# Slot rows stored by slot and gathered by token onto x, in place of scatter-adds into a copy of x

## The chip, the cores and the metric

The kernel runs on one core of a Trainium2 chip. The metric is the device time of one launch in microseconds; smaller is better. The core's engines run side by side and are tied by semaphores: TensorE (PE), VectorE (DVE), ScalarE (ACT), GpSimd (POOL) and SyncE (SP), which here only issues DMAs. ACT and POOL issue DMAs too; only POOL can issue indexed ones and ones that add to their destination.

## The reference

Four layers, each added to x (2048 tokens of 512 values, float32) through a gate:

```python
x = x + tanh(g_xattn[0]) * L0_xattn(layernorm(x), ids, ctx)      # per token one of 4 experts
x = x + tanh(g_ffn[0])   * L0_ffn(layernorm(x), w_gate, w_up, w_down)  # quantized FFN
x = x + tanh(g_xattn[1]) * L1_xattn(layernorm(x), ctx, ctx, gamma)
x = x + tanh(g_ffn[1])   * L1_ffn(layernorm(x), ...)             # 64 experts, top 6
```

The first layer picks an expert e by token id; with h = layernorm(x) it gives silu(h ctx[e]^T) * (h ctx[e]^T) ctx[e]^T for that token. The second quantizes activations and weights in blocks of 32 to a tiny float with a shared exponent. The change touches the end of the first layer and the start of the second. The third and fourth stay as they are.

## The kernel before

**Layer 1, in slots.** The tokens are sorted by expert into 19 slots of 128 rows; a slot belongs to one expert, and the last rows of an expert's last slot can be empty. DVE computes slot[p, i], the slot row of token 128 i + p, and token[p, j], the token of row p in slot j. For each slot j: POOL gathers the tokens' rows of x into hin (gather(j), L593, five slots ahead); DVE measures them (L907); POOL makes the deviations (L600 to L602); ACT normalises; TensorE turns them (turn_h, L1284) and multiplies by ctx (z, L1295); ACT's silu and DVE's product give prod (L913); TensorE turns it (turn_a, L1304) and multiplies again (y, L1311); ACT scales the result into ysb (L1662, signals y_out). POOL then scatters ysb to DRAM (scatter(j), L624): an indirect DMA that adds the 128 rows to x_sum, a tensor of 2048 + 19 x 128 rows. Its first 2048 rows are a copy of x, made by four DMAs on ACT's queue (L1690) at 24 us; empty rows go to the rest, by the index tile target, which DVE makes after token (five small instructions).

**The weights of layer 2** are quantized in the same slots, as 16 tiles; a slot j with j % 4 != 3 has one. SP loads a tile (load_w, L491 to L493, three DMAs of 256 KB, two tiles ahead, after POOL's wy_ready); DVE finds the largest values (L871) and the scales (L877, L880); POOL multiplies (normal, L608); ACT squares (L1668); DVE pushes and pulls (L886 to L898); TensorE turns the tile (turn_w, L1321); ACT writes it to SLAB.

**Hand-over.** When all scatters have landed, SP loads x_sum's first 2048 rows as 16 DMAs of 256 KB into X (L512). X held ctx until about 18 us and is free in between.

**Layer 2, in 16 tiles of tokens.** enter(i) measures X[i] on DVE (L949), deviation_x makes the deviations on POOL (L647 to L650, four small instructions), ACT normalises (L1717), measure_h finds the block scales on DVE (L957 to L959), and POOL's normal_h (L655), DVE's cast (L965) and POOL's back_h (L660) quantize. TensorE turns (L1358) and multiplies (L1366). The product's two halves h are quantized too: measure_i on DVE (L979 to L981), normal_i on POOL (L665), cast_i on DVE (L986), back_i on POOL (L671), then TensorE turns them (L1377) and multiplies down (L1385); DVE's leave adds to X (L991).

The order on each engine is the order in which the code is written; an engine waits at each instruction for its semaphores, and nothing behind it can overtake. POOL's order in step i of layer 2 is back_i(i-1,1), back_h(i+1), deviation_x if i is odd (up to i = 11), normal_i(i,0), normal_h(i+2), back_i(i,0), normal_i(i,1).

## Time and profile before

| | us |
|---|---|
| median of 3 runs | 1050.43 (1050.4 to 1052.26) |
| the profiled execution | 1051.51, of which span 1049.8 |
| PE busy | 973.2 (93%) |
| POOL busy | 639.8 (61%) |
| DVE busy | 632.5 (60%) |
| ACT busy | 420.8 (40%) |
| slots of layer 1 | about 24 to 205 |
| layer 2 | about 210 to 435 |

An engine's share is a mean over stages with different limits. A row of the timeline gives the start and the duration of an instruction (or of several of one kind), its engine and line, what it writes and reads, and in brackets how long the engine was idle before it and what ended that. A DMA's row on its issuing engine is the time to issue it; its landing is told apart. For POOL that time is the making of its descriptors.

### The profile page before, as it was taken

The page shows a single profiled execution, that of the slowest core. Times are in us where ns is not written, and L with a number is a line of the kernel's source. Part 1 is how long each engine was busy: PE and PEld are TensorE (multiplying, and loading weights), DVE is VectorE, ACT ScalarE, POOL GpSimd, SP SyncE. Part 2 cuts the span into 40 slices and gives each one's busy share as a digit, 9 for nine tenths or more (in the row PEclk, how much of TensorE's full clock was granted, in tenths as well). Part 3 has the DMA queues.
Part 4 walks back from the last instruction along what each step waited for, and adds up shares of the span by engine and source line. Part 5 has one row for each costly group of instructions (what it writes and reads, how often), then busy time and mean ns, then how long its engine had stood idle before and what let it go on. Part 6 is the DMA issues. An engine that isn't in the chain of part 4 may idle for free.

```text
span 1049.8 us, 13677 instructions
## 1 busy us (share of the span) xinstructions
PE 973.2 (93%) x4436; PEld 474.9 (45%) x4436; DVE 632.5 (60%) x1168; ACT 420.8 (40%) x817; POOL 639.8 (61%) x565
## 2 busy tenths in 40 slices
PE   6699999969999999799999999999999999999992
PEld 4355555424444444344444445335455555555530
DVE  5478876868888887577777777981222222222221
ACT  4466565434444444466666665332111111111100
POOL 4399996558888887686766661245444554445430
PEclk9899999989999999899999999999999999999996
DMA  9555555240000001230001605178999999999848
GB/s 310 190 131 142 122 144 115 48 143 1 1 1 1 2 1 41 81 130 21 21 23 36 234 1 201 30 259 272 331 336 333 340 335 335 338 335 334 242 63 182
DMA packets 64148, 162.90 MB, mean 155 GB/s; under 512 B 9888, under 2 KB 10032, under 8 KB 63632
## 3 DMA queue, kind: packets, MB, share of 16 engines
q1 hardware_dynamic: 47488, 116.94, 31.9%
q0 software_dynamic: 16464, 40.91, 18.1%
q10 hardware_dynamic: 128, 4.19, 1.2%
q8 instruction: 37, 0.61, 0.2%
q14 instruction: 31, 0.25, 0.1%
HBM read 129.67 MB, written 39.67 MB: 161 GB/s over the span
## 4 chain that ended last, share of the span: by engine, by line
PE 64%; POOL 14%; DVE 8%; issue 7%; DMA 4%; ACT 2%; SPq 0%; POOLq 0%; DVEq 0%; ACTq 0%
PE PS L1580 15%; PE PS L1599 8%; PE PS L1424 6%; PE PS L1401 6%; PE PS L1412 6%; POOL ARENA L665 6%; PE PS L1311 5%; PE PS L1295 5%; POOL ARENA L671 3%; PE PS L1569 3%; PE PS L367 3%; DVE ARENA L986 2%; POOL ARENA L660 1%; DMA XNT<-in_L_ffn_w_down 1%; DVE ARENA L1195 1%
## 5 line engine op out<-in xcount | busy, mean ns | idle before, releaser
L715 POOL TENSOR_TENSOR ARENA<-ARENA 128x512 f32<-128x512 f32 x128 | 133.3, 1063 | 55.8 <-DVE ARENA L1021 55.7
L1366 PE MATMUL PS<-SLAB,ARENA 128*128 128x512 bf16 x512 | 118.8, 382 | 12.6 <-DVE ARENA L972 10.9
L761 POOL DMA_INDIRECT out<-ARENA,idx x32 | 46.2, 1445 | 124.4 <-DVE ARENA L1227 106.8
L1855 ACT ACTIVATE ARENA<-PS 96x192 f32<-96x192 f32 x64 | 20.9, 327 | 226.4 <-PE PS L1580 186.3
L1227 DVE COPY ARENA<-PS 96x512 f32<-96x512 f32 x64 | 41.1, 682 | 94.6 <-PE PS L1599 94.6
L1762 ACT ACTIVATE ARENA<-PS,ARENA 128x512 f32<-128x512 f32 x128 | 86.8, 683 | 23.1 <-DVE ARENA L1015 19.8
L1015 DVE TENSOR_REDUCE ARENA<-PS 128x2 f32<-128x1024 f32 x64 | 78.2, 1222 | 9.3 <-PE PS L1401 9.1
L1366 PEld LDWEIGHTS PS<-SLAB,ARENA 128*128 128x128 bf16 x512 | 48.4, 98 | 75.0 <-issue 21.5
L1580 PE MATMUL PS<-SLAB,ARENA 128*96 128x384 f32 x240 | 81.0, 490 | 0.0
L1412 PEld LDWEIGHTS PS<-ident,ARENA 128*128 128x128 f32 x512 | 54.8, 141 | 51.1 <-issue 36.6
L1728 ACT ACTIVATE ARENA<-PS 128x512 f32<-128x512 f32 x64 | 38.2, 597 | 97.5 <-PE PS L1366 97.5
L671 POOL TENSOR_TENSOR ARENA<-ARENA 128x1024 bf16<-128x1024 fp8e4 x32 | 61.1, 1911 | 24.3 <-DVE ARENA L986 24.3
L665 POOL TENSOR_TENSOR ARENA<-ARENA 128x1024 f32<-128x1024 f32 x32 | 62.8, 1962 | 20.0 <-DVE ARENA L981 20.0
L754 POOL DMA_INDIRECT ARENA<-rows,idx x64 | 60.3, 942 | 23.3 <-issue 11.0
L1401 PE MATMUL PS<-ARENA 64*128 64x512 f32 x256 | 73.6, 652 | 0.2 <-ACT ARENA L1762 0.2
L1311 PE MATMUL PS<-CT,XNT 128*128 x152 | 70.9, 610 | 2.2 <-ACT XNT L1657 1.7
L1412 PE MATMUL PS<-ident,ARENA 128*128 128x128 f32 x512 | 70.7, 280 | 1.7 <-DVE XNT L1028 1.7
L1295 PE MATMUL PS<-CT,ARENA 128*128 x152 | 68.5, 593 | 1.6 <-ACT ARENA L1647 1.6
L1424 PE MATMUL PS<-XNT,CT 128*64 128x512 f32 x256 | 68.2, 616 | 0.0
L1215 DVE SCALAR_TENSOR_TENSOR ARENA<-PS,ARENA 96x192 f32<-96x192 f32 x64 | 26.2, 409 | 69.2 <-ACT ARENA L1855 62.8
L1385 PE MATMUL PS<-SLAB,ARENA 128*128 128x512 bf16 x256 | 62.0, 387 | 0.0
L1771 ACT ACTIVATE XNT<-PS 128x512 f32<-128x512 f32 x64 | 38.2, 597 | 53.2 <-PE PS L1412 53.1
(267 smaller groups left out, 1868.3 us busy)
## 6 DMA issues: line engine op xcount, KB each, us to landing
SLAB<-in_L_ffn_w_gate SPq DMA_DIRECT2D x30, 384.0 KB
SLAB<-in_L_ffn_w_up SPq DMA_DIRECT2D x30, 384.0 KB
X<-in_L_ffn_w_down SPq DMA_DIRECT2D x14, 768.0 KB
SLAB<-in_L_ffn_w_down SPq DMA_DIRECT2D x10, 768.0 KB
CT<-in_L_ffn_w_gate SPq DMA_DIRECT2D x16, 384.0 KB
CT<-in_L_ffn_w_up SPq DMA_DIRECT2D x16, 384.0 KB
X<-in_ctx SPq DMA_DIRECT2D x4, 1024.0 KB, 5.5
XNT<-in_L_ffn_w_gate SPq DMA_DIRECT2D x16, 256.0 KB
```

Of the source, the lines that this page charges most:

```text
L665: pool.tensor_tensor(blocks(iy[:, h, :]), blocks(inter[:, par, h, :]), spread(iinv[:, h, :]), ALU.mult).then_inc(iy_ready, 1)
L671: pool.tensor_tensor(blocks(qi[:, par, h, :]), blocks(ic[:, h, :]), spread(im[:, par, h, :]), ALU.mult).then_inc(iq_ready, 1)
L715: last = pool.tensor_tensor(prob[s % 4][:, h, :], prob[s % 4][:, h, :], rec[:, s % 4, h:h + 1].to_broadcast([P, D]), ALU.mult)
L1295: last = pe.matmul(bank(2 + j % 2), hT[:, j % 2, k * P:(k + 1) * P], CT[:, bass.ds(e, 1), k, :].rearrange("p a s -> p (a s)"), start=(k == ...
L1311: last = pe.matmul(bank(4 + j % 2), aT[:, j % 2, k * P:(k + 1) * P], CT[:, bass.ds(e, 1), k, :].rearrange("p a s -> p (a s)"), start=(k == ...
L1366: last = pe.matmul(bank(b), QT[:, par, k * P:(k + 1) * P], w[:, k, c * D:(c + 1) * D], start=(k == 0), stop=(k == KD - 1))
L1401: last = pe.matmul(bank(2 * (s % 2) + h), qn[rows_h, i % 2, c * P:(c + 1) * P], keys4[rows_h, i % 4, :], start=True, stop=True)
L1412: last = pe.transpose(bank(4 + h)[:, k * P:(k + 1) * P], prob[s % 4][:, h, k * P:(k + 1) * P], ident[:, :])
L1424: last = pe.matmul(bank(6 + i % 2)[h * DH:h * DH + DH, :], CT[:, b, k, r * P + h * DH:r * P + h * DH + DH], PT[h][i % 2][:, k, :], start=( ...
L1580: last = pe.matmul(bank(2 + e % 2)[0:CAP, 0:2 * F1].rearrange("p (n f) -> p n f", n=2), bT[:, e % 2, k, :], gate_up_of(e)[:, :, k, :], sta ...
L1599: last = pe.matmul(bank(4 + n)[0:CAP, :], hT6[half, t % 2, m, :], down_of(t)[half, m, :], start=(m == 0), stop=(m == 2))
L1762: last = act.activation(prob[s % 4][:, h, :], bank(2 * (s % 2) + h), ACT.Exp, bias=nmax[:, s % 4, h:h + 1], accum_out=esum[:, s % 4, h:h + 1])
```

## The change

- x_sum becomes slot_out, a tensor of 19 x 128 rows in the order of the slots. The copy of x on ACT's queue goes, and so do target, pads and target_ready.
- SP stores each slot's ysb to slot_out with a plain DMA (store_y). The store of slot j-1 stands in SP's order behind the weight tile of slot j; behind it stands the weight tile of slot j+1.
- SP loads x itself into X, eight DMAs of 512 KB, in slots 1 to 8.
- POOL's scatters go from the slots. After its last weight tile POOL waits for X and all stores and gathers slot_out by slot[:, i] onto X[:, i, :] with an indirect DMA that adds (gather_x): four at once, number 4 before normal_h(0), number 5 before normal_h(1), then two at the end of each of the steps 0 to 4.
- The matmuls that find token have 38 columns in place of 57.

The weight tiles stay in the slots in which they were.

```diff
+                def store_y(j):
+                    sp.wait_ge(y_out, j + 1)
+                    sp.dma_start(slot_out_v[:, j, :], ysb[:, j % 2, :]).then_inc(y_stored[j % 2], 16)
+
                 for j in range(SLOTS):
                     if j in TILED and tile_at(j) + 2 < NT:
                         load_w(tile_at(j) + 2)
-
-                sp.wait_ge(y_stored[0], 16 * ((SLOTS + 1) // 2))
-                sp.wait_ge(y_stored[1], 16 * (SLOTS // 2))
-                for i in range(NT):
-                    need(sp, yg_in[i % 4], 16 * (i // 4))
-                    sp.dma_start(X[:, i, :], x_sum_v[:, i, :]).then_inc(yg_in[i % 4], 16)
+                    if 1 <= j <= NT // 2:
+                        need(sp, c_turned, NT)
+                        sp.dma_start(X[:, 2 * j - 2:2 * j, :], x_v[:, 2 * j - 2:2 * j, :]).then_inc(x_in, 16)
+                    if j:
+                        store_y(j - 1)
+                store_y(SLOTS - 1)
...
-                    pool.indirect_dma_start(x_sum, bass.IndirectOffsetOnAxis(ap=target[:, j:j + 1], axis=0),
-                                            ysb[:, j % 2, :], None, compute_op=ALU.add).then_inc(y_stored[j % 2], 16)
...
+                def gather_x(i):
+
+                    need(pool, yg_in[i % 4], 16 * (i // 4))
+                    pool.indirect_dma_start(X[:, i, :], None, slot_out, bass.IndirectOffsetOnAxis(ap=slot[:, i:i + 1], axis=0),
+                                            compute_op=ALU.add).then_inc(yg_in[i % 4], 16)
+
+                pool.wait_ge(x_in, 16 * (NT // 2))
+                pool.wait_ge(y_stored[0], 16 * ((SLOTS + 1) // 2))
+                pool.wait_ge(y_stored[1], 16 * (SLOTS // 2))
+                for i in range(4):
+                    gather_x(i)
                 deviation_x(0, 1)
                 deviation_x(1, 1)
+                gather_x(4)
                 normal_h(0)
                 back_h(0, 0)
                 deviation_x(2, 2)
+                gather_x(5)
                 normal_h(1)
...
                     if live(i, 0):
                         back_i(i, 0, par)
                         normal_i(i, 1, par)
+                    for g in range(2 * i + 6, min(2 * i + 8, NT)):
+                        gather_x(g)
...
-                for b in range(B):
-                    act.dma_start(x_sum[b * S:(b + 1) * S, :], x_rows[b * S:(b + 1) * S, :]).then_inc(x_in, 16)
```

SP's order in slots 1 to 3. In the kernel before, weight tiles 3, 4 and 5 follow each other (L491 to L493, here tile 3 and the first DMA of tile 4):

```order
L491 DMA XNT<-in_L_ffn_w_gate 128x512
L492 DMA XNT<-in_L_ffn_w_up 128x512
L493 DMA XNT<-in_L_ffn_w_down 128x512
L491 DMA XNT<-in_L_ffn_w_gate 128x512
L492 DMA XNT<-in_L_ffn_w_up 128x512
```

After the change, from tile 3 on (L512 loads x, L505 stores a slot):

```order
L489 DMA XNT<-in_L_ffn_w_gate 128x512
L490 DMA XNT<-in_L_ffn_w_up 128x512
L491 DMA XNT<-in_L_ffn_w_down 128x512
L512 DMA X<-in_x 128x2x512
L505 DMA slot_out<-ARENA 128x512
L489 DMA XNT<-in_L_ffn_w_gate 128x512
L490 DMA XNT<-in_L_ffn_w_up 128x512
L491 DMA XNT<-in_L_ffn_w_down 128x512
L512 DMA X<-in_x 128x2x512
L505 DMA slot_out<-ARENA 128x512
L512 DMA X<-in_x 128x2x512
L505 DMA slot_out<-ARENA 128x512
```

Between two weight tiles there is now a load of x and one or two stores, each store with a wait for y_out.

POOL's order in step 0 of layer 2 and the head of step 1, before: normal_i(0,0), normal_h(2), back_i(0,0), normal_i(0,1), back_i(0,1), back_h(2).

```order
L665 TENSOR_TENSOR ARENA<-ARENA 128x1024
L655 TENSOR_TENSOR ARENA<-ARENA 128x512
L671 TENSOR_TENSOR ARENA<-ARENA 128x1024
L665 TENSOR_TENSOR ARENA<-ARENA 128x1024
L671 TENSOR_TENSOR ARENA<-ARENA 128x1024
L660 TENSOR_TENSOR ARENA<-ARENA 128x512
```

The same place after the change (normal_i is L655 there, normal_h L645, back_i L661, back_h L650, gather_x L667):

```order
L655 TENSOR_TENSOR ARENA<-ARENA 128x1024
L645 TENSOR_TENSOR ARENA<-ARENA 128x512
L661 TENSOR_TENSOR ARENA<-ARENA 128x1024
L655 TENSOR_TENSOR ARENA<-ARENA 128x1024
L667 DMA X<-slot_out,slot 128x512 x2
L661 TENSOR_TENSOR ARENA<-ARENA 128x1024
L650 TENSOR_TENSOR ARENA<-ARENA 128x512
```

Two gathers now stand between normal_i(0,1) and back_i(0,1); steps 1 to 4 have the same.

## Rows read from the trace of the kernel before

**Rows 1.** Busy time by stretch: engines with counts, PE clock, DMA share, GB/s.

```profile
core 0: us, PE busy (x) PEld busy (x) DVE busy (x) ACT busy (x) POOL busy (x), PEclk, DMA share, GB/s
60.00:70.00 10.00, 10.00 (x56) 6.05 (x55) 7.61 (x8) 7.08 (x12) 9.05 (x8) 1.00 0.58 155
```

**Rows 2.** The chain of waits, slots 1 and 2: start us, us, what.

```profile
52.13 4.65 PE PS L1311 x8
56.78 3.43 PE PS L1295 x8
60.22 0.44 PE PS L1304 x4
...
61.76 3.49 PE PS L1311 x8
```

**Rows 3.** Timeline of DVE around weight tiles 1 and 2.

```profile
24.92 1.75 DVE L871 TENSOR_REDUCE ARENA<-XNT 128x48 f32<-128x1536 f32 x1 [4.00 <-DMA XNT<-in_L_ffn_w_down]
...
29.65 0.19 DVE L880 TENSOR_SCALAR ARENA<-ARENA 128x48 int16<-128x48 int16 x1
42.42 1.75 DVE L871 TENSOR_REDUCE ARENA<-XNT 128x48 f32<-128x1536 f32 x1 [12.58 <-DMA XNT<-in_L_ffn_w_down]
```

**Rows 4.** Timeline of SP's queue: first DMA of tile 1, last of tile 2.

```profile
18.33 0.33 SPq L491 DMA_DIRECT2D XNT<-in_L_ffn_w_gate  x1
...
27.07 0.49 SPq L493 DMA_DIRECT2D XNT<-in_L_ffn_w_down  x1
```

**Rows 5.** DMA queues from 20 to 45 us: packets, MB, share of 16 engines.

```profile
q10 hardware_dynamic: 128, 4.19, 49.4%
```

**Rows 6.** Timeline of TensorE, the turns of prod(1).

```profile
45.62 1.11 PE L1304 MATMUL PS<-ident,XNT 128*128 128x128 f32 x4 [4.13 <-DVE XNT L913]
```

**Rows 7.** Timeline of POOL, steps 4 and 5 of layer 2.

```profile
279.49 1.92 POOL L665 TENSOR_TENSOR ARENA<-ARENA 128x1024 f32<-128x1024 f32 x1 [1.09 <-DVE ARENA L981]
...
285.33 2.02 POOL L665 TENSOR_TENSOR ARENA<-ARENA 128x1024 f32<-128x1024 f32 x1 [0.39 <-DVE ARENA L981]
288.16 1.91 POOL L671 TENSOR_TENSOR ARENA<-ARENA 128x1024 bf16<-128x1024 fp8e4 x1 [0.81 <-DVE ARENA L986]
...
292.72 1.92 POOL L665 TENSOR_TENSOR ARENA<-ARENA 128x1024 f32<-128x1024 f32 x1
```

**Rows 8.** Timeline, slots 2 to 4: a weight load, y_out(2), DVE's next measurement.

```profile
63.06 0.33 SPq L491 DMA_DIRECT2D XNT<-in_L_ffn_w_gate  x1
...
65.89 0.70 ACT L1662 ACTIVATE ARENA<-PS,tgate 128x512 f32<-128x512 f32 x1
...
75.85 0.69 DVE L907 BATCH_NORM_STATS2 ARENA<-ARENA 128x6 f32<-128x512 f32 x1 [2.08 <-DMA ARENA<-in_x,ARENA]
```

**Rows 9.** Lines 593 (gathers) and 624 (scatters): POOL's time and the landing.

```profile
L593 POOL DMA_INDIRECT ARENA<-in_x,ARENA x19: 945/1032/2610, 14.4 to 158.0; - x19
...
DMA to landing us min/median/max: 4.2/5.4/6.2
...
L624 POOL DMA_INDIRECT x_sum<-ARENA x19: 1585/1663/3264, 54.0 to 201.8; - x19
...
DMA to landing us min/median/max: 4.7/6.0/7.3
```

**Rows 10.** Timeline of the hand-over: last y_out, first enter, first measure_h.

```profile
200.79 0.70 ACT L1662 ACTIVATE ARENA<-PS,tgate 128x512 f32<-128x512 f32 x1
...
210.25 0.69 DVE L949 BATCH_NORM_STATS2 ARENA<-X 128x6 f32<-128x512 f32 x1 [3.81 <-DMA X<-x_sum]
...
213.64 0.69 DVE L957 TENSOR_REDUCE ARENA<-ARENA 128x16 f32<-128x512 f32 x1
```

**Rows 11.** Line 549, twelve plain stores of 256 KB from X to DRAM: landing.

```profile
DMA to landing us min/median/max: 2.0/2.4/3.0
```

**Rows 12.** Line 789, direct DMAs of 256 rows that add, on POOL.

```profile
L789 POOL DMA_DIRECT2D out<-SLAB x2: 1182/1206/1231, 1032.0 to 1035.1; - x2
```

**Rows 13.** Timeline of DVE beside the first scatter.

```profile
53.93 1.75 DVE L886 SCALAR_TENSOR_TENSOR ARENA<-ARENA,XNT 128x1536 f32<-128x1536 bf16 x1
```

**Rows 14.** Timeline of TensorE, the last turns of layer 2, after a wait each.

```profile
425.29 0.62 PE L1377 MATMUL PS<-ident_b,ARENA 128*128 128x128 bf16 x8 [2.09 <-POOL ARENA L671]
...
430.30 1.03 PE L1377 MATMUL PS<-ident_b,ARENA 128*128 128x128 bf16 x8 [2.89 <-POOL ARENA L671]
```

More of the change, by code:

```diff
@@ L102, in build @@
     slot_in = nc.dram_tensor("slot_in", [SLOTS * P, D], F32, kind="Internal").ap()
[L103 removed]
+    slot_out = nc.dram_tensor("slot_out", [SLOTS * P, D], F32, kind="Internal").ap()
     rows = nc.dram_tensor("rows", [ROWS, RW], F32, kind="Internal").ap()
@@ L236, in build @@
         x_rows = x.rearrange("b s d -> (b s) d")
-        x_sum_v = x_sum[0:T, :].rearrange("(i p) d -> p i d", p=P)
+        slot_out_v = slot_out.rearrange("(j p) d -> p j d", p=P)
         def blocks(a, n=BLK):
@@ L639, in _ @@
                     normal(n)
-                scatter(SLOTS - 1)
                 def deviation_x(i, n):
```

24 lines of the change are left out of this document (3 added, 21 removed).

## The prediction

> **What bounds the kernel now.** I read the busy table in slices of 10 us first, then the chain of waits from 0 to 300 us, then the timelines of the engines at the places where the chain leaves TensorE. Only the first 430 us matter: what follows does not touch x_sum, the scatters or X's loading, and moves as a block. All times below are on the clock of the kernel before.
>
> The expert slots (24 to 205 us) are bound by TensorE once they run: it is busy 10.00 of 10 us, at full clock, while DVE has 7.61 and the DMA engines 0.58 [rows 1]. A full slot of the chain is z (3.43), four turns of prod and h (0.44 each), twelve of the weight tile and y (3.49) [rows 2]. Before they run there is one stall. DVE is free at 29.84 and its next instruction, the largest values of weight tile 2 (L871), begins at 42.42, after 12.58 us of idle that ended with the tile's DMA [rows 3]. The last of its three DMAs was issued at 27.07 [rows 4]. Between 20 and 45 us the copy of x into x_sum (queue q10, 4.19 MB) held 49.4% of the 16 engines, 12.4 us of 25 [rows 5]. TensorE waits from 45.62 - 4.13 = 41.49, the end of z(2), for prod(1), which stands behind L871 on DVE [rows 6]; it then waits again for the tile's own transposes. Its matmuls after that run slowly: y(1) takes 4.65 us where a later y takes 3.49 [rows 2].
>
> In the quantized FFN (218 to about 425 us) the chain of waits goes POOL, DVE, POOL. In a step, normal_i(i,0) (L665), back_i(i,0), normal_i(i,1), back_i(i,1) (L671) are tied by a DVE cast or measurement between each two. The last of these gaps is 0.81 us on POOL [rows 7]. back_i(i,1) is issued at the head of step i+1, and behind it stand back_h, four small instructions if i+1 is odd, and normal_i(i+1,0). With the four small ones POOL comes to normal_i(i+1,0) without a gap (292.72); without them it waits 1.09 us (279.49) [rows 7]. So time put on POOL between normal_i(i,1) and back_i(i,1) is hidden for 0.81 us if i is even, for 0.81 + 1.09 = 1.90 us if it is odd, and lengthens the FFN beyond that.
>
> **Part 1, the copy of x goes (gain).** Four DMAs leave ACT's queue. x now comes to SBUF as eight loads of 512 KB in slots 1 to 8. Weight tile 2 is asked for from 26.1 on and then lands by 33: tile 1 was asked for at 18.33 and used at 24.92, 6.6 us later, with five gathers beside it [rows 3, 4]. TensorE ends z(2) at 41.49 and goes on: 41.49 + (61.76 - 60.22 = 1.54 of turns) = 43.03, where y(1) begins, + 3.49 = 46.53, where z(3) begins. DVE does not hold it: from L871 to y(1) all that hangs on tile 2 took 52.13 - 42.42 = 9.71 us [rows 2, 3], and 33 + 9.71 = 42.7. Before, z(3) begins at 56.78 [rows 2]. Gain 10.25 us, of which 1.2 is the y at full clock. Each us by which tile 2 lands after 33.3 costs one; I take 9 to 10.5 as bounds. The slots behind it are tied to TensorE and keep the gain.
>
> The X loads use the same engines. A slot's share is 0.58 now [rows 1]; they add at most 12.4 / 8 = 1.5 us of engine time to each of eight slots of 3.43 + 3.49 + 1.54 = 8.46 us, 0.18, and the scatters leave. So nothing waits there. The Trainium skill (DMA: Bandwidth & Descriptors, Issuing engines are not separate DMA queues) says the same of the mechanism: transfers from SP, ACT and POOL run on the same engines and interleave. By it the 12.4 us of engine time are only moved, and the sum would lose what part of them meets a busy engine.
>
> **Part 2, scatters become stores.** Nineteen scatters leave POOL's slot stage (1.59 to 3.26 us each [rows 9]); POOL is not on the chain there, 0. Each store is now an SP instruction that waits for y_out(j), and behind it stand the next three weight DMAs. After a slot without a tile the load is then later than today: SP issues at 63.06, while y_out of slot 2 comes at 65.89 + 0.70 = 66.59 [rows 8]. Tile 5 lands some 3.5 us later, about 1 us behind the time DVE takes it; DVE then idles 2.08 us in that slot anyway [rows 8]. Four such slots: 0, with 4 x 0.5 as the bad bound. Five small DVE instructions and a third of the columns of the matmuls at 13 us leave as well; DVE then waits 2 us for tile 0 anyway: 0.
>
> **Part 3, the hand-over.** Before, y_out(18) ends at 200.79 + 0.70 = 201.49, its scatter and X's first load follow, and DVE measures tile 0 at 210.25 and begins measure_h(0) (L957) at 213.64 [rows 10]. After: SP issues the store at about 201.6; a 256 KB store lands in 2.4 us (2.0 to 3.0) [rows 11], 204.0. Then POOL issues four gathers that add into X.
>
> **What is such a gather's price?** The trace has no gather with an add. Plain gathers of the same 128 rows cost POOL 0.945 at least, 1.03 in the median; scatters with the add 1.585 at least, 1.66 in the median. They land in 4.2 to 6.2 and 4.7 to 7.3 us [rows 9]. A direct DMA with the add costs 1.2 [rows 12]. I take 1.60, since it is the row with both properties, indexed and adding; 1.03 stays the low end. Landing 4.7. Between two of them stand 0.3 us, as between two plain ones.
>
> Gather 3 is issued at 204.0 + 3 x 1.9 = 209.7 and lands at 214.4; enter(3) takes 0.9, so measure_h(0) begins at 215.3: 1.7 us later than before. With 1.03 and 4.2 it is 204.0 + 4.0 + 4.2 + 0.9 = 213.1, 0.5 earlier; with 1.66 and 7.3, 4.5 later. POOL's two deviations wait behind the gathers but end before measure_h(0). Gathers 4 and 5 fall where POOL waits in any case: 0.
>
> **Part 4, ten gathers inside FFN steps 0 to 4.** Each of these steps has two, right before back_i(i,1). A pair costs 0.17 + 1.60 + 0.30 + 1.60 + 0.07 = 3.74. Steps 0, 2 and 4 hide 0.81: 3 x 2.93 = 8.8. Steps 1 and 3 hide 1.90: 2 x 1.84 = 3.7. Sum 12.5 us. TensorE waits for back_i(i,1) with its transposes, has nothing to do meanwhile, and the stage never gets it back, since later steps have the same tie. With 1.03 a pair is 2.60: 3 x 1.79 + 2 x 0.70 = 6.8. With 2.2 (a DVE instruction beside it) it is 4.94: 3 x 4.13 + 2 x 3.04 = 18.5.
>
> On that last price: the first scatter, at 54.0, is the longest, 3.26 us in place of 1.60 [rows 9], and beside it runs a DVE instruction with two inputs in SBUF (L886) [rows 13]. The Trainium skill (SBUF — State Buffer, Who interferes with whom) has the rule: DVE and GpSimd hold a shared port pair exclusively, and a DMA issued from GpSimd can't write its descriptors meanwhile. The rows agree. By that rule the casts beside a pair could cost a gather up to their own length. In the FFN, DVE has one cast beside a pair and no instruction like L886; I take nothing for it in the sum.
>
> **Sum.** -10.25 + 1.7 + 12.5 = +3.95 us. The profiled execution took 1051.51 (span 1049.8), 1.1 above the median of 1050.43; the change is made against itself, so 1050.4 + 4.0 = **1054.4 us**.
>
> **The rivals.**
> (a) The gather is cheap. It counts as a gather, not as a scatter: 1.03 to 1.2 us. Then -10.25 - 0.5 + 6.8 = -3.95 at 1.03, 1046.5 us; at 1.2 (pair 2.94: 3 x 2.13 + 2 x 1.04 = 8.5, hand-over +0.3) it is -1.5, 1049. This one ends faster. It decides below 1.15 us a gather. For it: plain gathers hardly grow with rows, and a direct add of 256 rows costs 1.2 [rows 12]. Against it: the only indexed adds in the trace are the dear ones.
> (b) The clock falls. After a wait of 2.89 us in TensorE, eight transposes took 1.03 us, after one of 2.09 only 0.62 [rows 14]; a pair of gathers leaves it about 3 us without work. With the 1.16 us that y(1) lost to the same cause, a fallen clock costs some 0.41 + 1.16 = 1.6 us a step, less what the chain covers (up to 0.8). In three to five steps 3 to 7 us on top of the forecast: 1057 to 1061.
> (c) The front stays. If tile 2 still lands at 42 or another wait takes L871's place (an SP wait, a gather of h), part 1 gives nothing or half: 1059 to 1065. The timeline speaks against it: all else that DVE and TensorE need then is there by 38.
>
> **Chances.** Forecast (1052.5 to 1057.5) 0.40; (a) 0.42, of which 0.24 with 1.03 and 0.18 with 1.2; (b) 0.12; (c) 0.06. So the forecast is the likeliest of the prices. A difference of 0.2%, 2.1 us, is about what a measurement of this kernel can tell from none. Faster by more than that: 0.32, nearly all of (a) at 1.03, a third of (a) at 1.2; within it 0.21, the rest of (a) and the forecast's low edge; slower 0.47. The range runs from the low end of (a), with another 1.5 us for the front, to the middle of (b) and of the cheaper (c): 1045.0 to 1060.0; the forecast's own is 1052.5 to 1057.5.
>
> **What the profile after would show.** Right: no wait of DVE for tile 2 over 3 us, TensorE busy without a hole from 34 us on, z(3) about 10 us earlier; POOL's DMA_INDIRECT into X near 1.6 us; measure_h(0) 8.5 us earlier than 213.64, not 10; back_i(i,1) behind two gathers in five steps, periods near 16 and 14.6 us there in place of 13.2 and 12.7. Wrong: gathers near 1.0 (then a); L1377 at 1.0 in steps 1 to 5 (then b); a wait of 5 us or more in TensorE before 60 (then c), or TensorE waiting for tiles 5, 8, 11 or 14, which would make the SP order dear.

## The result, and the profile after

| | before | after |
|---|---|---|
| median of 4 runs each, us | 1051.35 (1050.4 to 1052.29) | 1060.13 (1059.27 to 1060.85) |
| the profiled execution, us | 1051.51 | 1059.75 |
| its span, us | 1049.8 | 1057.8 |
| ratio of the runs, 95% interval | | 1.0075 (1.0062 to 1.0088) |

The changed kernel is slower, by 8.0 us of span, 8.2 us of profiled time and 8.8 us between the medians (7.9 us by the ratio); the forecast was +3.95. The sign and the mechanism came as forecast, and the size is twice that.

**The front.** The timeline of DVE after, the largest values of weight tiles 1, 2 and 3 (start us, us, what; in brackets the idle time before and what ended it):

```profile
24.70 1.75 DVE L869 TENSOR_REDUCE ARENA<-XNT 128x48 f32<-128x1536 f32 x1 [3.64 <-DMA XNT<-in_L_ffn_w_down]
31.80 1.75 DVE L869 TENSOR_REDUCE ARENA<-XNT 128x48 f32<-128x1536 f32 x1 [1.35 <-DMA XNT<-in_L_ffn_w_down]
40.37 1.75 DVE L869 TENSOR_REDUCE ARENA<-XNT 128x48 f32<-128x1536 f32 x1
```

The second row is tile 2: it waited 1.35 us where [rows 3] show 12.58. TensorE then has no hole (timeline of TensorE, y(1) and z(3)):

```profile
43.48 3.65 PE L1309 MATMUL PS<-CT,XNT 128*128 x8
46.97 3.60 PE L1293 MATMUL PS<-CT,ARENA 128*128 x8
```

z(3) begins 9.81 us earlier than in [rows 2]. The gain is kept: y_out(18) ends at 191.14 + 0.70 = 191.84 us, 9.65 before that of [rows 10].

**The hand-over.** POOL, DVE and TensorE in order of time: the four gathers (L667), the last enter, measure_h(0) (L955), the first turns and products of the FFN (L1356, L1364) and the first normal_i (L655):

```profile
194.65 1.85 POOL L667 DMA_INDIRECT X<-slot_out,slot  x1 [6.37 <-DMA slot_out<-ARENA]
...
200.53 1.54 POOL L667 DMA_INDIRECT X<-slot_out,slot  x1 [0.30 <-issue]
...
205.98 0.69 DVE L947 BATCH_NORM_STATS2 ARENA<-X 128x6 f32<-128x512 f32 x1 [1.36 <-DMA X<-slot_out,slot]
...
206.81 0.65 DVE L955 TENSOR_REDUCE ARENA<-ARENA 128x16 f32<-128x512 f32 x1
...
210.65 0.61 PE L1356 MATMUL PS<-ident_b,ARENA 128*128 128x128 bf16 x4 [7.68 <-POOL ARENA L650]
212.04 9.69 PE L1364 MATMUL PS<-SLAB,ARENA 128*128 128x512 bf16 x32 [0.78 <-ACT ARENA L1719]
...
222.09 1.91 POOL L655 TENSOR_TENSOR ARENA<-ARENA 128x1024 f32<-128x1024 f32 x1 [5.21 <-DVE ARENA L979]
```

measure_h(0) is 6.83 us earlier than in [rows 10], so the hand-over took 2.8 of the 9.65. normal_i(0,0) is only 5.55 earlier (227.64 before): another 1.3 went in the first products, which took 9.69 us in place of 8.38.

**The steps.** POOL in step 0 and at the head of step 1: normal_i(0,1), the pair of gathers, back_i(0,1), back_h(1), and, behind four small instructions, normal_i(1,0):

```profile
227.93 2.02 POOL L655 TENSOR_TENSOR ARENA<-ARENA 128x1024 f32<-128x1024 f32 x1 [0.39 <-DVE ARENA L979]
230.10 2.04 POOL L667 DMA_INDIRECT X<-slot_out,slot  x1 [0.15 <-issue]
232.44 1.55 POOL L667 DMA_INDIRECT X<-slot_out,slot  x1 [0.30 <-issue]
233.43 2.51 POOL L661 TENSOR_TENSOR ARENA<-ARENA 128x1024 bf16<-128x1024 fp8e4 x1
235.30 1.64 POOL L650 TENSOR_TENSOR ARENA<-ARENA 128x512 bf16<-128x512 fp8e4 x1
...
238.64 1.90 POOL L655 TENSOR_TENSOR ARENA<-ARENA 128x1024 f32<-128x1024 f32 x1
```

normal_i(i,0) begins at 222.09, 238.64, 252.95, 269.85, 284.17 and 300.85 us, so the five steps take 16.55, 14.31, 16.90, 14.32 and 16.68 us, where they took 13.25, 12.67, 13.24, 12.69 and 13.23: +13.7 in all. Shift by shift: -9.65 at y_out(18), -6.83 at measure_h(0), -5.55 at normal_i(0,0), +8.1 at normal_i(5,0), +8.0 at the end. From step 5 on the kernel moves as a block but for small shifts that cancel: +6.9 behind the end of layer 2, where the last sixteen products down took 5.27 us before and 4.45 after (TensorE's granted clock was 0.70 in the kernel before from 433 to 439 us), and +8.0 again at the end.

(The start that the trace gives a POOL instruction right behind a gather is too early: L661 "begins" at 233.43 while the gather runs to 233.99. Its end, 235.94, fits the instructions behind it. So sums over steps go by ends or by rows further on. Two of the starts above, 252.95 and 284.17, are of this kind: the instructions last 2.5 us there and 1.9 elsewhere. By the ends of normal_i(i,0) the five steps are longer by 3.3, 2.2, 3.1, 2.2 and 2.8 us.)

### The profile page after: what moved, and what is told of

The parts are those of the page before. It is cut to its first block, busy times and chain, and to the rows that moved or that the text cites. A ratio compares the mean times of both kernels' runs of the same rounds, so it can differ in the third digit from the quotient of the medians.

```text
span 1057.8 us, 13675 instructions
## 1 busy us (share of the span) xinstructions
PE 973.7 (92%) x4436; PEld 475.7 (45%) x4436; DVE 632.3 (60%) x1163; ACT 420.0 (40%) x817; POOL 631.8 (60%) x562
## 4 chain that ended last, share of the span: by engine, by line
PE 65%; POOL 15%; DVE 7%; issue 7%; DMA 2%; ACT 2%; POOLq 0%; DVEq 0%; ACTq 0%; SPq 0%
PE PS L1578 15%; PE PS L1597 8%; PE PS L1293 6%; PE PS L1422 6%; PE PS L1399 6%; PE PS L1410 6%; PE PS L1309 6%; POOL ARENA L655 6%; POOL ARENA L661 4%; PE PS L1567 3%; PE PS L365 3%; DVE ARENA L984 2%; POOL X L667 2%; POOL ARENA L650 1%; DVE ARENA L1193 1%
## 5 line engine op out<-in xcount | busy, mean ns | idle before, releaser
L1364 PE MATMUL PS<-SLAB,ARENA 128*128 128x512 bf16 x512 | 119.6, 385 | 10.5 <-DVE ARENA L970 8.8
L1364 PEld LDWEIGHTS PS<-SLAB,ARENA 128*128 128x128 bf16 x512 | 49.0, 99 | 72.8 <-issue 19.0
L611 POOL TENSOR_TENSOR XNT<-XNT,ARENA 128x1536 f32<-128x1536 f32 x16 | 45.6, 2851 | 52.3 <-DVE ARENA L878 52.1
L661 POOL TENSOR_TENSOR ARENA<-ARENA 128x1024 bf16<-128x1024 fp8e4 x32 | 63.5, 1986 | 20.5 <-DVE ARENA L984 20.5
L655 POOL TENSOR_TENSOR ARENA<-ARENA 128x1024 f32<-128x1024 f32 x32 | 63.9, 1998 | 17.2 <-DVE ARENA L979 17.2
L759 POOL DMA_INDIRECT ARENA<-rows,idx x64 | 60.0, 938 | 23.7 <-issue 11.3
L1383 PE MATMUL PS<-SLAB,ARENA 128*128 128x512 bf16 x256 | 64.9, 400 | 0.0
```

Of the source, the lines that this page charges most:

```text
L655: pool.tensor_tensor(blocks(iy[:, h, :]), blocks(inter[:, par, h, :]), spread(iinv[:, h, :]), ALU.mult).then_inc(iy_ready, 1)
L661: pool.tensor_tensor(blocks(qi[:, par, h, :]), blocks(ic[:, h, :]), spread(im[:, par, h, :]), ALU.mult).then_inc(iq_ready, 1)
L1364: last = pe.matmul(bank(b), QT[:, par, k * P:(k + 1) * P], w[:, k, c * D:(c + 1) * D], start=(k == 0), stop=(k == KD - 1))
```

## The experiments

Each is compared with the kernel before on the same chip at the same time. One thing must be known to read the profiled times: z(0), the first product, takes 3.69 us in some executions and 5.39 in others, whatever the kernel. In the long ones TensorE's granted clock falls to half during it (0.50 from 25 to 28 us in the profile of the copy by rows, 1.00 throughout in that of the kernel before). Of the thirteen profiles, seven have 5.39, and all that follows in them is 1.7 us later. The kernel before was profiled with 3.69, the changed kernel too. It may be what sets the two levels of the runs of before (1050.4 and 1052.3); that was not shown.

### Part 1 by itself

The kernel before without the copy and with scatters that write:

```diff
-                for b in range(B):
-                    act.dma_start(x_sum[b * S:(b + 1) * S, :], x_rows[b * S:(b + 1) * S, :]).then_inc(x_in, 16)
...
-                                            ysb[:, j % 2, :], None, compute_op=ALU.add).then_inc(y_stored[j % 2], 16)
+                                            ysb[:, j % 2, :], None).then_inc(y_stored[j % 2], 16)
```

> The kernel before without the copy of x and with scatters that write in place of adding (it leaves out the addition of x to the first layer's result). All else stands. This is part 1 of the prediction by itself. Theory: -9.7 to -10.3 from the front, nothing else on the path but the last scatter, which without the add costs POOL about 0.5 us less: 1051.3 - 10 - 0.5 = 1040.8, bounds 1039.5 to 1042.5. Rival (the front gains less than 9 us, the rest of the changed kernel's loss being smaller than I read it): 1043 to 1047. The price of a scatter without add: 0.95 to 1.1 us if the add is what is dear, 1.6 if it is the direction.

Measured: 1039.14 us against 1053.02, ratio 0.9871 (0.9854 to 0.9887), 13.9 us faster, more than I had expected (my lower bound was 1039.5). Its timelines:

```profile
46.93 3.60 PE L1294 MATMUL PS<-CT,ARENA 128*128 x8
...
192.07 1.93 POOL L623 DMA_INDIRECT x_sum<-ARENA  x1 [3.83 <-ACT ARENA L1661]
...
202.38 0.65 DVE L956 TENSOR_REDUCE ARENA<-ARENA 128x16 f32<-128x512 f32 x1
```

z(3) at 46.93 is that of the changed kernel (46.97), and so is the last y_out, whose instruction on ACT begins at 191.10 (191.14). So the front of the change is the copy and nothing else, -9.7 us. Of the rest I had expected 0.5 us: measure_h(0) is 11.3 us earlier than in [rows 10], 1.6 more than the front. A scatter that writes lands sooner: SP, which waits for it, issues X's first load 195.77 - 192.07 = 3.70 us after the scatter began, in place of 207.36 - 201.76 = 5.60. POOL's part of that is 1.93 us in place of 2.51; the remainder, 1.77 in place of 3.09, is on the way to memory. So at this place adding costs there too, not only on POOL. The profiled span gained 12.6 us: 11.3 up to normal_i(5,0) (281.45 in place of 292.72), and most of the other 1.3 at the end of layer 2, in the products at a lower clock named above.

The price of a scatter without the add was to be read here as well. The quickest took 1.01 us on POOL in place of 1.585, so the add is what is dear in this direction too. But the median was 1.93, more than the 1.66 of the scatters with the add [rows 9]: in the slots what runs beside a scatter counts for more than the add.

### The price of the add

The changed kernel, with gathers that overwrite:

```diff
-                    pool.indirect_dma_start(X[:, i, :], None, slot_out, bass.IndirectOffsetOnAxis(ap=slot[:, i:i + 1], axis=0),
-                                            compute_op=ALU.add).then_inc(yg_in[i % 4], 16)
+                    pool.indirect_dma_start(X[:, i, :], None, slot_out, bass.IndirectOffsetOnAxis(ap=slot[:, i:i + 1], axis=0)).then_inc(yg_in[i % 4], 16)
```

> The changed kernel, with the sixteen gathers of slot_out writing X in place of adding to it (it leaves out the addition of x after the first layer). Everything else stands. Theory (the add is the price): POOL needs 1.0 to 1.1 us a gather in place of 1.57, as for the plain gathers of h; a step with a pair gets 1.0 to 1.3 us shorter, the hand-over 1.5 to 2.5: 1060.1 - 5 x 1.15 - 2 = 1051.5 to 1054.5. Rival (the indexed read into X or the place in the program is the price): gathers stay at 1.5 or more, 1059 to 1061.

Measured: 1050.14 us against 1052.36, ratio 0.9988 (0.9977 to 0.9999), some 9 to 10 us under the changed kernel and 1.4 under my range. Line 667 (POOL's time min/median/max in ns, then the landing) in the changed kernel, and then in this one:

```profile
L667 POOL DMA_INDIRECT X<-slot_out,slot x16: 1539/1568/2112, 194.7 to 294.7; - x16
...
DMA to landing us min/median/max: 4.6/5.0/5.7
```

```profile
L667 POOL DMA_INDIRECT X<-slot_out,slot x16: 946/1035/1525, 194.5 to 285.3; - x16
...
DMA to landing us min/median/max: 3.4/3.6/4.0
```

The add costs 0.53 us of POOL and 1.4 us of landing for each gather. This is the point on which the forecast and rival (a) parted: with the price of a plain gather (1.03) the change would have been about level with the kernel before. The two terms shrink where they should: the five steps lengthen by 7.35 us in place of 13.7, and normal_i(0,0) comes at 218.78, 3.3 us earlier. I had given the hand-over 1.5 to 2.5 us of this; that the landing gets shorter as well I had left out.

### Part 4 by itself

The changed kernel without the ten late gathers (DVE's enter waits for x alone from tile 6 on):

```diff
-                    for g in range(2 * i + 6, min(2 * i + 8, NT)):
-                        gather_x(g)
```

> The changed kernel without the ten gathers of steps 0 to 4 (it leaves out the first layer's result for tiles 6 to 15); the six before the FFN stay. Theory: all of the lengthening of steps 0 to 4 (3.30, 1.64, 3.66, 1.63, 3.45 us, 13.7 in all) is the gathers on POOL: 1060.1 - 13.7 = 1046.4, with 1045.5 to 1047.5 as bounds, periods of 13.2 and 12.7 us, and a full TensorE clock from 225 us on. Rival (part of it is TensorE's fallen clock from the hand-over, or DMA traffic, which stays without them): 1048 to 1052.

Measured: 1046.38 us against 1052.36, ratio 0.9940 (0.9920 to 0.9960). Against the changed kernel's 1.0075 that is 1.35%, 14.2 us, and the spans differ by 14.1 (its z(0) took 5.39 us, its first products 8.57 in place of 9.69, so the gathers' price is better read from the periods). POOL's normal_i(i,0) begins at 222.77, 236.04, 248.70, 262.11, 274.78 and 288.01: periods of 13.27, 12.66, 13.41, 12.67 and 13.23, those of the kernel before within 0.2 us in all. So the 13.7 us are the gathers.

### Where in a step POOL's time is free

The ten late gathers one to a step, the same number at the same place:

```diff
-                    for g in range(2 * i + 6, min(2 * i + 8, NT)):
-                        gather_x(g)
+                    if i + 6 < NT:
+                        gather_x(i + 6)
```

> The changed kernel, with the ten late gathers one to a step (number i + 6 at the end of step i, steps 0 to 9) in place of two in steps 0 to 4. The number of gathers, their price and their place in a step are the same. Theory (each step hides what POOL waits anyway before back_i(i,1) and, if i is odd, before the next normal_i as well: 0.81 and 1.90 us): one gather with its gaps is 1.84 (2.3 where it takes 2.04); five even steps cost 1.03 to 1.5 each, five odd ones 0 to 0.4. So +5.2 to +9.5 in place of +13.7: 1051.6 to 1056, best 1052.5. Rival (ten gathers cost what they cost, nothing is hidden): 1060. Second rival (shorter waits of TensorE also keep its clock full): up to 1 us less than the theory's sum.

Measured: 1054.00 us against 1053.02, ratio 1.0010 (1.0001 to 1.0020). Nearly 7 us of the ten gathers' cost is gone, with all ten still there. The even steps and the odd ones part as the model has it (POOL, the gathers of steps 0 to 2 and normal_i(i,0) of steps 0 to 3):

```profile
223.94 1.91 POOL L655 TENSOR_TENSOR ARENA<-ARENA 128x1024 f32<-128x1024 f32 x1 [5.49 <-DVE ARENA L979]
...
231.96 2.04 POOL L667 DMA_INDIRECT X<-slot_out,slot  x1
238.65 1.90 POOL L655 TENSOR_TENSOR ARENA<-ARENA 128x1024 f32<-128x1024 f32 x1
...
246.69 2.10 POOL L667 DMA_INDIRECT X<-slot_out,slot  x1 [0.18 <-issue]
251.31 2.30 POOL L655 TENSOR_TENSOR ARENA<-ARENA 128x1024 f32<-128x1024 f32 x1
...
259.72 1.60 POOL L667 DMA_INDIRECT X<-slot_out,slot  x1 [0.15 <-issue]
265.97 1.90 POOL L655 TENSOR_TENSOR ARENA<-ARENA 128x1024 f32<-128x1024 f32 x1
```

A pair of steps takes 265.97 - 238.65 = 27.32 us from an odd step's head on, where it took 25.9. Two gathers of 2.10 and 1.60 with their gaps are 4.2 us of POOL, and 2.71 (0.81 + 1.90) of that is hidden: 1.5 is left, 1.4 measured. The rival (a gather costs what it costs) is out.

### The clock at the head of the FFN

Five more matmuls that nobody reads:

```diff
-                unread(6)
+                unread(11)
```

> The changed kernel, with five more of the matmuls that nobody reads (L1325, 0.43 us each) after the last weight tile, so that TensorE is idle 5.5 us before the first transposes of the FFN, as in the kernel before (5.18), and not 7.68. Theory (the 1.3 us that the first step lost come from the clock, which rises later: gate_up of tile 0 took 9.69 us in place of 8.38): gate_up(0) back to 8.4 us, normal_i(0,0) 1.3 us earlier, 1058.8. Rival (gather 5, which stands between the deviations and normal_h(1), is what delays the first step, and the clock is no cause): 9.69 stays or falls without any gain, 1060.1.

Measured: 1059.91 us against 1053.02, ratio 1.0062 (1.0037 to 1.0086). The theory (1058.8 in place of 1060.1) stood for a ratio near 1.0062 and the rival for 1.0075. The interval holds both, so the times decide nothing.

The trace of the changed kernel decides on the rival. The first transposes were released by back_h(0,0), which ended at 210.60, before gather 5 began (212.50); TensorE was busy without a gap in the products; and normal_i(0,0) followed their end by 0.36 us, as in the kernel before. Gather 5 held up nothing here. The 1.3 us are TensorE's clock, which the changed kernel shows as follows (length, busy TensorE, its granted clock in shares of 2.4 GHz, DMA share, GB/s):

```profile
208.00:209.00 1.00, 0.00 (x0) 0.50 0.84 135
...
216.00:217.00 1.00, 1.00 (x4) 0.50 0.63 113
217.00:218.00 1.00, 1.00 (x5) 0.81 0.00 0
218.00:219.00 1.00, 1.00 (x7) 1.00 0.00 0
```

Whether a longer wait cost more of it is another matter. This is what the thirteen profiles have (TensorE's idle time before the FFN's first transposes, these four transposes, and the 32 products behind; where one of the products is missing from the trace, 31):

| kernel | wait, us | transposes, us | products, us |
|---|---|---|---|
| last slot sooner (below) | 1.01 | 0.40 | 6.85 (31) |
| DVE adding out of PSUM (below) | 2.64 | 0.40 | 8.54 (31) |
| no copy | 3.55 | 0.40 | 8.27 |
| five more matmuls (this run) | 3.85 | 0.40 | 8.18 (31) |
| rows of x kept (below) | 4.26 | 0.61 | 9.30 (31) |
| overwriting gathers | 4.41 | 0.45 | 9.93 |
| before | 5.18 | 0.61 | 8.38 |
| copy behind the tile (below) | 5.29 | 0.60 | 9.55 |
| copy by rows (below) | 5.43 | 0.61 | 9.97 |
| after | 7.68 | 0.61 | 9.69 |
| six gathers | 7.98 | 0.61 | 8.57 |
| one gather a step | 8.04 | 0.61 | 9.60 (31) |
| direct adds (below) | 8.50 | 0.60 | 8.89 (31) |

From 4.26 us on the length says nothing: the products take 8.4 to 10.0 us in no order, and two kernels that are the same up to this place, with waits of 7.98 and 8.04 us, took 8.57 and 9.60. In the three profiles with waits of 2.64 to 3.85 us the transposes still ran at full clock; the clock fell to half behind them, and the products took 8.2 to 8.5. After 1.01 us it didn't fall at all. So the 1.3 us lie within what this place varies by from profile to profile, and that the longer wait of the changed kernel caused them is not shown. Nor is it refuted: this run's edit brought the wait to 3.85 us, and its products are among the quick ones.

### Why the copy held weight tile 2

Two versions of the kernel before that keep copy, scatters and hand-over. The first names the rows:

```diff
-                    act.dma_start(x_sum[b * S:(b + 1) * S, :], x_rows[b * S:(b + 1) * S, :]).then_inc(x_in, 16)
+                    act.dma_start(x_sum_v[:, 4 * b:4 * b + 4, :], x_v[:, 4 * b:4 * b + 4, :]).then_inc(x_in, 16)
```

> The kernel before, with one edit: the four DMAs of the copy of x name their rows (128 x 4 rows of 2 KB each) in place of one contiguous MB each. In the kernel before the copy went as 128 packets of 32 KB, the weight tile beside it in packets of 2 KB. Theory (packet size): an engine takes the queues in turn, one packet each, so a weight row waits for a 32 KB packet each time; with packets of 2 KB tile 2 gets its share, lands by about 33 us, and DVE's wait for it falls from 12.58 us to under 4. Then TensorE goes on as in the changed kernel, and the time is 8 to 10 us under the kernel before: 1041.5 to 1043.5. Rival (bytes): 4.2 MB ahead of the tile keep the engines full for 12 us however they are cut; the wait stays at 9 to 12.6 us and the time at 1048 to 1052. A second rival: the copy by rows is itself slower and scatter 0 waits for it on POOL, which gives part of the gain back: 1044 to 1048.

Measured: 1046.32 us against 1052.36, ratio 0.9944 (0.9928 to 0.9961). DVE's row for tile 2 and the queues from 20 to 46 us (packets, MB, share of 16 engines), first before, then here:

```profile
q10 hardware_dynamic: 128, 4.19, 47.5%
q1 hardware_dynamic: 1295, 2.36, 26.5%
```

```profile
37.49 1.75 DVE L871 TENSOR_REDUCE ARENA<-XNT 128x48 f32<-128x1536 f32 x1 [5.82 <-DMA XNT<-in_L_ffn_w_down]
...
q10 hardware_dynamic: 2112, 4.19, 47.5%
q1 hardware_dynamic: 1292, 2.35, 26.3%
```

The copy took the same share of the engines, but tile 2 landed 10.3 us after its last issue in place of 15.3. DVE's wait fell from 12.58 us to 5.82, where it is 1.35 without a copy: packets of 2 KB in place of 32 KB give back six tenths of the stall. The rest stays, which speaks for the bytes. Neither theory was right alone. The time lies in the range of the second rival, but not for its reason: POOL issued scatter 0 after 0.17 us of idle time, so it didn't wait for the copy, though the copy's four DMAs landed later (13.6 us in the median in place of 10.0). As a change to the kernel this line gives 6 us at no cost.

The second moves the copy behind tile 2 on SP's queue:

```diff
                         load_w(tile_at(j) + 2)
+                    if j == 0:
+                        for b in range(B):
+                            sp.dma_start(x_sum[b * S:(b + 1) * S, :], x_rows[b * S:(b + 1) * S, :]).then_inc(x_in, 16)
```

> The kernel before, with the same copy of x (contiguous, 32 KB packets) issued by SP right behind weight tile 2 on SP's queue, not by ACT ahead of it. It takes the front of the change alone: scatters, x_sum and the loads of X by SP stay. Theory: tile 2 lands before 33 us, DVE's wait for it is under 4 us, TensorE has no hole at 41 us; but tile 3, asked for near 33 us, now stands behind the copy until about 43, some 3 us later than DVE wants it, and scatter 0 holds POOL until the copy has landed. Gain 6 to 9.5: 1042 to 1045.5. Rival (the stall only moves to tile 3 or to POOL behind scatter 0): gain 0 to 4, 1047 to 1051.

Measured: 1049.32 us against 1052.36, ratio 0.9968 (0.9955 to 0.9980). Tile 2 came in time, and tile 3, which now stood behind 4 MB, became the stall:

```profile
31.86 1.75 DVE L874 TENSOR_REDUCE ARENA<-XNT 128x48 f32<-128x1536 f32 x1
...
48.98 1.75 DVE L874 TENSOR_REDUCE ARENA<-XNT 128x48 f32<-128x1536 f32 x1 [7.12 <-DMA XNT<-in_L_ffn_w_down]
```

Its last DMA landed 13.4 us after its issue. The rival had this right: most of the stall only moves.

### Towards a kernel that is faster than both

The front gives 9.7 us and the ten gathers take more than that back. Four kernels try to have the first without the second.

**Scatters that write, then eight direct adds.** X is loaded from x in the slots, POOL scatters by token without add, and adds x_sum's rows onto X by ordinary DMAs of 256 rows:

```diff
+                def add_y(g):
+                    need(pool, yg_in[g % 4], 16 * (g // 4))
+                    pool.dma_start(X[:, 2 * g:2 * g + 2, :], x_sum_v[:, 2 * g:2 * g + 2, :], accum_op=ALU.add).then_inc(yg_in[g % 4], 16)
```

> Half of each kernel: no copy of x, SP loads x into X in slots 1 to 8 as in the changed kernel; POOL scatters each slot by token as in the kernel before, but without the add (nothing has to be there first); after the last one POOL adds the rows onto X with eight direct DMAs of 256 rows (two at once, one before normal_h(0), one before normal_h(1), one at the end of steps 1, 3, 5 and 7). Theory (an add of 256 contiguous rows costs POOL 1.2 us as at the kernel's end, 1.7 beside a cast of DVE, and odd steps hide 1.9): front -9.6 and hand-over -1.9 as in the kernel without the copy, +2 to +4 for the add in place of SP's load, 0 in the steps: 1052.5 - 13.9 + 3 = 1041.6, bounds 1039.5 to 1044. Rival (the add itself lands late, 8 to 12 us as the two at the kernel's end, 11.4 to 12.0 us): the hand-over loses 6 to 9 us, 1045 to 1048.

Measured: 1047.63 us against 1051.62, ratio 0.9962 (0.9948 to 0.9976). The steps cost nothing, as expected: normal_i(1,0) at 238.70, (2,0) at 251.37, (3,0) at 264.62, with an add of 1.26 us in step 1. The loss is at the hand-over: the adds were issued at 199.67, DVE had tile 0 only at 205.87, 6.2 us later, and tile 2 at 208.96. From the last scatter's start to measure_h(0) it took 15.2 us, 4.9 more than with SP's loads in the kernel without the copy. That is less than the rival's 6 to 9 and more than my 2 to 4; the time is in the rival's range.

**The rows of x kept in SBUF.** Each slot's rows of x are gathered anyway, for the normalisation. Here they go into X, which is free, and stay there; no copy of x is needed, since POOL adds them onto ysb before a scatter that writes:

```diff
-                    pool.indirect_dma_start(hin[:, j % HR, :], None, x_rows,
+                    pool.indirect_dma_start(X[:, j % NT, :], None, x_rows,
...
+                    own.link(pool.tensor_tensor(ysb[:, j % 2, :], ysb[:, j % 2, :], X[:, j % NT, :], ALU.add))
                     pool.indirect_dma_start(x_sum, bass.IndirectOffsetOnAxis(ap=target[:, j:j + 1], axis=0),
-                                            ysb[:, j % 2, :], None, compute_op=ALU.add).then_inc(y_stored[j % 2], 16)
+                                            ysb[:, j % 2, :], None).then_inc(y_stored[j % 2], 16)
```

> The kernel before, without the copy of x: each slot's rows of x are gathered into X (free until the hand-over) and stay there; ACT normalises from X into hin; POOL adds them onto ysb (128 x 512, some 1.05 us) and scatters without add into x_sum; SP loads X at the hand-over as before. Theory (the copy is the whole cost of the front, and an indirect DMA without add is cheap on POOL in this direction too, 0.95 to 1.1 us): DVE's wait for tile 2 under 3.5 us, z(3) near 47, so -9.7; POOL has in a slot 2.76 + 1.05 + 1.05 + 1.07 + 1.0 = 6.9 of 8.46 us, so the slots stay bound by TensorE; the last scatter comes 1.1 us later and costs 0.5 less. 1051.3 - 9.7 + 0.6 = 1042.2, with 1040.5 to 1044 as bounds: faster than both kernels. Rival (POOL becomes the bound of the slots with a tile, since its gathers and adds run beside DVE instructions that hold it up): 0.5 to 1 us a slot, 1047 to 1055.

Measured: 1058.26 us against 1053.02, ratio 1.0044 (1.0029 to 1.0058), slower, and above even the rival's range of 1047 to 1055. The rival had the mechanism and too small a price (0.5 to 1 us a slot): POOL became the bound of a slot with a tile, 10.87 us where TensorE needs 8.46:

```profile
66.61 2.76 POOL L609 TENSOR_TENSOR XNT<-XNT,ARENA 128x1536 f32<-128x1536 f32 x1
69.33 2.78 POOL L624 TENSOR_TENSOR ARENA<-ARENA,X 128x512 f32<-128x512 f32 x1
72.40 2.30 POOL L625 DMA_INDIRECT x_sum<-ARENA  x1 [0.29 <-POOL ARENA L624]
...
77.47 2.76 POOL L609 TENSOR_TENSOR XNT<-XNT,ARENA 128x1536 f32<-128x1536 f32 x1
```

The addition takes 1.26 us in a slot without a tile (at 61.36) and 2.78 here, and the scatter 1.10 and 2.30. Beside them run DVE's instructions with two inputs in SBUF, one of which is itself held up (2.70 us, where it takes 1.76 alone):

```profile
71.02 2.70 DVE L893 SCALAR_TENSOR_TENSOR ARENA<-ARENA 128x1536 bf16<-128x1536 bf16 x1
```

**The same, with DVE adding out of PSUM.** ACT's scaling and POOL's addition become one instruction:

```diff
+                    dve.scalar_tensor_tensor(out=ysb[:, j % 2, :], in0=bank(4 + j % 2), scalar=tgate[:, 0:1], in1=X[:, j % NT, :],
+                                             op0=ALU.mult, op1=ALU.add).then_inc(y_out, 1)
```

> The kernel in which each slot's rows of x stay in X, with one edit: DVE makes ysb = gate x y + x out of PSUM in one instruction a slot (some 0.75 us), in place of ACT's scaling and POOL's addition. Theory (what made that kernel slow was POOL: its addition took 2.78 us and its scatter 2.30 beside DVE's two-input instructions, 10.87 us a slot with a tile in place of 8.46): POOL is back to 2.76 + 2.3 + 1.2 + 1.2 = 7.5 us a slot, and DVE has 8.7 + 0.75 = 9.45 us in a slot with a tile and 2.3 in one without, 30.6 in four slots of 33.8: 1041 to 1043.5 if its lag within the three is hidden. Rival (TensorE waits for DVE in each slot with a tile, by up to 1 us in three of four): +4 to +10, 1046 to 1052.

Measured: 1043.49 us against 1051.62, ratio 0.9928 (0.9905 to 0.9951): faster than both kernels. TensorE is busy 126.1 of 130 us between 60 and 190 (128.3 in the kernel before). DVE's lag in three slots with a tile is nearly hidden, but not at the end of the slots. There the last slot's instruction stood behind a cast that POOL held up:

```profile
189.93 3.00 DVE L895 TENSOR_SCALAR ARENA<-ARENA 128x1536 bf16<-128x1536 bf16 x1
192.96 0.96 DVE L898 TENSOR_TENSOR ARENA<-ARENA 128x1536 bf16<-128x1536 bf16 x1
193.84 0.75 DVE L918 SCALAR_TENSOR_TENSOR ARENA<-PS,tgate,X 128x512 f32<-128x512 f32 x1
```

**The last slot sooner.** One instruction moved:

```diff
+                    if last:
+                        slot_out(SLOTS - 1)
                     dve.wait_ge(wc_ready, n + 1)
```

> The kernel in which DVE makes ysb out of PSUM and the rows of x kept in X, with one edit: the last slot's instruction stands between two parts of the last slot's weight tile (behind L892, in front of L895) in place of behind all four. Theory: y(18) was ready on TensorE at 191.7 us, but DVE made it at 193.84, behind a cast (L895) that POOL's long multiplication held up for 3.0 us; now it is made by 192.5 and its scatter goes out as soon as POOL has ended that multiplication, at 192.6 in place of 194.86. The hand-over is 1.3 to 2.2 us earlier: ratio to the kernel before 0.9910 (0.9890 to 0.9925). Rival (DVE's own rest, which ends at 199.6 and is pushed back by what it waits for y(18), takes the place): no change, 0.9928.

Measured: 1040.81 us (1039.94 to 1041.58) against 1052.32, ratio 0.9890 (0.9873 to 0.9906). This is the best version: 11.5 us faster than the kernel before and, by the two ratios, 1.85% or some 19 us faster than the changed one.

The expected way of the gain doesn't show in the profile. POOL scatters y(18) at 194.32, 0.5 us sooner, and needs 1.14 us in place of 2.27, so that SP's first load goes out 1.7 us sooner. But DVE's own rest is then the last thing before enter(0) at 201.14 (201.76 without the move), and measure_h(0) waits for ACT and begins at 205.47 (205.49). The first transposes come at 209.34 (209.32). At this point the rival was right: nothing was gained. The two profiles are fit to be compared here, since y(18) leaves TensorE at the same time in both; z(0) took 1.7 us longer in this one, and y(18) 1.7 longer in the other. What the profile of this kernel has is the stretch behind: TensorE ended its earlier work 1.6 us later, waited 1.01 us in place of 2.64, and did the products at full clock, in 6.85 us in place of 8.54. The later end goes back to the long z(0): POOL's last multiplication beside the slots began 1.7 us later too (190.62 in place of 188.96), ahead of anything that was moved. So this stretch is no proof for the move. The ratios (0.9890 against 0.9928) speak for a gain; its cause stays open.

```profile
209.34 0.40 PE L1368 MATMUL PS<-ident_b,ARENA 128*128 128x128 bf16 x4 [1.01 <-POOL ARENA L660]
210.74 6.85 PE L1376 MATMUL PS<-SLAB,ARENA 128*128 128x512 bf16 x31 [0.99 <-ACT ARENA L1731]
```

## Why the prediction was right, point by point

**What bounds the kernel** was read rightly in both places. The copy and only the copy made the stall at tile 2 (no copy: -9.7 us at z(3)), and the FFN's steps are lengthened by POOL's time between normal_i(i,1) and back_i(i,1) beyond 0.81 or 1.90 us (one gather a step, and no gathers).

**Part 1**, forecast -10.25 with bounds 9 to 10.5, came as -9.65. DVE's wait was under 3 us and z(3) 9.8 earlier. The start of the slots was 0.6 later (z(0) at 25.05 after 24.44), which is the difference; z(0) begins anywhere from 24.44 to 25.11 in the thirteen profiles, whatever the kernel. The 12.4 us of engine time that X's loads brought into the slots met nothing: TensorE kept its period of 8.46 us a slot (z(3) at 46.97, z(4) at 55.43), with the DMA engines at 0.72 from 60 to 70 us, where they had been at 0.58. The Trainium skill (DMA: Bandwidth & Descriptors, Issuing engines are not separate DMA queues) has all these transfers on the same engines; the part of the gain that the sum could have lost by that was not lost.

**Part 2**, forecast 0: the changed kernel's TensorE waited for a weight tile's transposes once between 30 and 190 us, 1.1 us, as it did in the kernel before between 60 and 200. DVE waited for tiles' DMAs 8.1 us in seven waits, none over 1.7, and TensorE saw none of it.

**Part 3**, forecast +1.7, came as +2.8. The store took 2.8 us with its issue in place of 2.5, the four issues 5.9 in place of 5.7, and the last gather 5.45 from its issue to enter(3) in place of 4.7: 1.2 us in three small terms. The landing was the term mis-sized: I took 4.7, the quickest of the scatters with the add, and the gathers with the add took 4.6 to 5.7. "Gathers 4 and 5: 0" held: gather 4 ended at 207.02, 0.95 us before normal_h(0) could begin, and gather 5 stands behind all that released the first transposes. The +1.3 in the first products had no term in the sum. It is TensorE's clock, and lies within what the clock's return varies by at this place.

**Part 4**, forecast +12.5, came as +13.7. The price of 1.60 was right (1.57 in the median), as was its reason, the add. What failed is the sentence "I take nothing for it in the sum". The first gather of a pair took 2.04, 2.10 and 2.11 us in steps 0, 1 and 3, and 1.57 in steps 2 and 4; the second took 1.55 or 1.56, and 1.79 in step 2. In the three, DVE's cast began 0.12 to 0.14 us ahead of it:

```profile
229.98 0.69 DVE L984 TENSOR_SCALAR ARENA<-ARENA 128x1024 fp8e4<-128x1024 f32 x1 [0.45 <-POOL ARENA L655]
...
292.79 1.57 POOL L667 DMA_INDIRECT X<-slot_out,slot  x1 [0.15 <-issue]
...
292.89 0.69 DVE L984 TENSOR_SCALAR ARENA<-ARENA 128x1024 fp8e4<-128x1024 f32 x1
```

The gather at 230.10 began inside the cast at 229.98 and took 0.5 longer, what was left of it. The gather at 292.79 began ahead of its cast and took 1.57. With one gather a step it is the same: the five in odd steps, each 0.14 or 0.15 us behind the start of a cast, took 2.10 or 2.11 us, and the even ones behind step 0, each 0.09 to 0.11 ahead of one, 1.59 or 1.60. Step 0's pair is then, from the end of normal_i(0,1) to back_i(0,1), 0.15 + 2.04 + 0.30 + 1.55 + 0.05 = 4.09, less 0.81 hidden: +3.28, and +3.30 was measured. The Trainium skill (SBUF — State Buffer, Who interferes with whom) has just this: whoever of the two engines issues first holds the shared ports for its whole instruction. By that a gather can lose at most the cast's own 0.69 us, and in these rows it loses less. I had read it and left it out of the sum.

**Rival (a)** fell on the price, by the row of line 667. **Rival (b)** came in part and cost next to nothing in the steps. TensorE's clock was 0.66 between 250 and 260 us, and TensorE was busy 7.36 of the 10. Step 1 shows the rival's sign, eight transposes in 1.04 us behind a wait of 3.56:

```profile
250.00:260.00 10.00, 7.36 (x31) 0.66 0.30 47
```

```profile
252.64 1.04 PE L1375 MATMUL PS<-ident_b,ARENA 128*128 128x128 bf16 x8 [3.56 <-POOL ARENA L661]
```

Yet the five steps add up from POOL's rows alone (step 1: 4.17 us from normal_i(1,1) to back_i(1,1), whose start is taken as its end less 1.91, are 2.3 beyond the hidden 1.90, and 2.2 were measured), and without the gathers the whole 13.7 is back. In steps 0, 2, 3 and 4 the eight transposes took 0.62 us, in step 3 behind a wait of 3.57, as long as that of step 1. So a wait of this length brings the rival's cost at times, and here POOL's chain covered it. **Rival (c)** did not come.

Altogether the forecast missed by 4.1 us of span, and its own range with it: 0.6 at the front, 1.1 at the hand-over, 1.3 in the first products and 1.2 in the steps, all on the same side. Each bound was given, but the likeliest value was put at the cheap end four times over, with the forecast's own range (1052.5 to 1057.5) as if the four could offset each other. The wide range, 1045.0 to 1060.0, was put on a base of 1050.4. On that base the measured ratio gives 1058.3, inside it; the median of 1060.13 stands at its very edge, as the kernel before had 1051.35 this time. And that it lies in the 1057 to 1061 of rival (b) is luck: the clock gave 1.3 us at the head of the FFN, where the rival did not look, and nothing measurable in the steps, where it had 3 to 7.

## What to carry to other kernels

- Work taken off an engine in a stage where it has time (POOL in the slots) and put on it in one where it is in the chain costs its full price there, less the gap that ends at that point. The gap is to be read for each place: the same ten gathers cost 13.7 us in pairs and about 7 one to a step.
- A large copy from DRAM to DRAM ahead of small loads that are needed soon holds them up by more than its share. Drop it, or at least cut it into packets of the loads' size.
- Data that has passed through SBUF anyway (here each slot's rows of x) can save both the copy and the add, if the addition goes to an engine that reads it out of PSUM, and not to two engines working side by side on SBUF.
